# TensorE picks 23 more of 832 gathered columns: a graph network kernel on one core of Trainium2

## The reference, cut to what matters

```python
msg = H[src] * norm[:, None]
out = jax.ops.segment_sum(msg, dst, num_segments=n)          # GCN, three times
...
msg = diff @ tw.T + tb + phi[dst]                            # diff = x[src] - x[dst]
agg = jax.ops.segment_max(msg, dst, num_segments=x.shape[0]) # edge convolution, four times
```

## Time and profile before

| | us |
|---|---|
| median of 3 runs | 9450.62 (9448.05 to 9455.34) |
| the profiled execution | 9444.14 |
| its span, first to last instruction | 9442.3 |

### The profile page before, as it was taken

The page is one execution under the profiler, slowest core; times in us unless marked ns, Lnnn a source line. Parts: engine busy times, 40 slices in busy tenths (PEclk is TensorE's granted clock), DMA queues, the critical chain, the costliest instruction groups (busy, mean ns, idle before and its releaser), DMA issues. The chain is left out here.

```text
span 9442.3 us, 137452 instructions
## 1 busy us (share of the span) xinstructions
PE 1819.4 (19%) x9607; PEld 1531.1 (16%) x9607; DVE 3654.1 (39%) x20408; ACT 3485.0 (37%) x23810; POOL 6987.7 (74%) x6815
## 2 busy tenths in 40 slices
PE   2000057788884000020002000020002000020000
PEld 1000046777774000010001000010001000010000
DVE  4333344444443333333333333333334333333333
ACT  4444221111114444334442444334442444324441
POOL 5777668888883777777777777777776777777777
PEclk6555567777777555565556555565555555555555
DMA  6444535555553333333333333333334333333333
GB/s 214 161 159 158 190 79 77 77 77 77 75 72 111 108 108 112 110 108 108 113 111 111 111 109 108 113 105 112 108 110 138 103 117 111 109 108 110 108 112 128
DMA packets 483882, 1071.04 MB, mean 113 GB/s; under 512 B 162484, under 2 KB 293278, under 8 KB 428104
## 3 DMA queue, kind: packets, MB, share of 16 engines
q0 software_dynamic: 310432, 442.95, 21.5%
q1 hardware_dynamic: 169557, 619.06, 17.8%
q10 hardware_dynamic: 2940, 1.00, 0.1%
HBM read 511.83 MB, written 559.14 MB: 113 GB/s over the span
## 5 line engine op out<-in xcount | busy, mean ns | idle before, releaser
L1035 POOL DMA_INDIRECT WORK<-table,S x5502 | 5194.3, 944 | 1923.2 <-issue 1689.0
L1071 DVE COPY FE<-XF 128x4 uint8 x9856 | 1311.1, 190 | 3271.9 <-issue 1824.8
L1114 ACT COPY FE<-XF 128x4 uint8 x20608 | 2101.3, 191 | 1104.6 <-issue 1092.0
L1134 ACT COPY WORK<-psum 128x512 f32<-128x512 f32 (+1 forms) x1456 | 846.3, 581 | 2874.1 <-DVE psum L1089 2864.6
L1304 POOL DMA_INDIRECT acc<-TOT,stage x832 | 1301.3, 1564 | 274.6 <-issue 209.7
L1089 DVE SCALAR_TENSOR_TENSOR psum<-psum,RESET,WORK 128x128 f32<-128x128 f32 x3320 | 1189.1, 358 | 493.3 <-DMA WORK<-table,S 426.8
L1154 PE MATMUL psum<-ident,FE 128*128 128x128 f32 x238 | 106.5, 447 | 6110.0 <-ACT FE L1114 4714.0
L1089 DVE SCALAR_TENSOR_TENSOR psum<-psum,KEEP,WORK 128x128 f32<-128x128 f32 x2490 | 896.9, 360 | 639.9 <-DMA WORK<-table,S 278.8
L1154 PEld LDWEIGHTS psum<-ident,FE 128*128 128x128 f32 x238 | 43.3, 182 | 6172.5 <-issue 5903.0
L1438 ACT COPY TOT<-psum 128x512 f32<-128x512 f32 x208 | 121.9, 586 | 1250.2 <-DMA acc<-TOT,stage 1245.0
L1509 DVE SCALAR_TENSOR_TENSOR BASE<-psum,WEIGHT,BASE 128x128 f32<-128x128 f32 x832 | 234.1, 344 | 761.9 <-PE psum L1379 761.8
(11 more groups left out here) (255 smaller groups left out, 2540.4 us busy)
## 6 DMA issues: line engine op xcount, KB each, us to landing
run_rows<-WORK SPq DMA_DIRECT2D x357, 1024.0 KB, 4.2
WORK<-table SPq DMA_DIRECT2D x10752, 0.5 KB
WORK<-table,S POOLq DMA_INDIRECT x5502, 2.6
fill_rows<-BASE SPq DMA_DIRECT2D x52, 1024.0 KB, 6.8
WORK<-fill_rows SPq DMA_DIRECT2D x104, 512.0 KB, 3.7
table<-TF SPq DMA_DIRECT2D x56, 384.0 KB
WORK<-carry_rows SPq DMA_DIRECT2D x49, 384.0 KB, 6.6
acc<-TOT,stage POOLq DMA_INDIRECT x832, 3.3
```

The lines of the kernel that those rows point to most:

```text
L1035: pool.indirect_dma_start(RING_T[:, b * WIDE + k, :], None, table, table_row(table, INDEX[:, t:t + 1]))\
L1071: i = dve.tensor_copy(PICKED[:, s, e:e + 1].bitcast(u8), TT[:, ds(held_rows["dve"][e % 32], 4)])
L1114: i = act.copy(PICKED[:, j % 2, e:e + 1].bitcast(u8), TT[:, ds(held_rows["act"][e % 32], 4)])
L1134: act.copy(RING_T[:, t % SPAN:t % SPAN + n, :], CHAINED[:, t % PSUM_COLS:t % PSUM_COLS + n, :])\
```

## The change

23 more columns (BY_PE: 63, 95, ... 767) leave GpSimd's list. TensorE makes them: for each edge a product of the identity with the column of `XF` at a register's address, whose 128 x 1 result goes into one column of bank 6 or 7. It does 16 edges per quad, 32 registers loaded at a time. When 128 are there (`built_p`), ScalarE copies the bank into `PICKED` (`drawn`), and from there the column goes the way of the other picked ones: a transpose, and ScalarE's copy into the ring. The transposes now use bank 5 alone, so that each waits for the copy of the one before it, and the chain's ring in PSUM shrinks from 24 to 20 columns. TensorE's loop now runs over the quads, with the picks of a quad ahead of the transposes that are due there. The edges' addresses of BY_PE are in units of float32 columns, not bytes.

```diff
-PSUM_COLS = 24
+PSUM_COLS = 20
...
-FROM_TT = sorted(BY_ACT + BY_DVE)
-AWAY = BY_ACT + BY_DVE + BY_SP
+BY_PE = [t for t in range(63, 772, 32)]
+FROM_TT = sorted(BY_ACT + BY_DVE + BY_PE)
+AWAY = BY_ACT + BY_DVE + BY_PE + BY_SP
...
-                for k, (t, size) in enumerate([(t, 4) for t in BY_ACT + BY_DVE] + [(t, 4 * F) for t in BY_SP]):
+                for k, (t, size) in enumerate([(t, 4) for t in BY_ACT + BY_DVE] + [(t, 1) for t in BY_PE] + [(t, 4 * F) for t in BY_SP]):
...
                 for q in range(quads):
                     pick_edges(q)
+                    for j, col in enumerate(BY_PE):
+                        if q == col // QUAD - 3:
+                            act.wait_ge(built_p, j + 1)
+                            wait(act, off_turned, FROM_TT.index(BY_PE[j - 2]) + 1 if j > 1 else 0)
+                            act.copy(PICKED[:, 4 + j % 2, :], bank(6 + j % 2)[:, 0:P]).then_inc(drawn, 1)
                     for j, col in enumerate(FROM_TT):
                         if q == col // QUAD - 2:
                             c = col // WIDE
                             act.wait_ge(off_turned, j + 1)
                             wait(act, stored[c % RING], c // RING * 16)
-                            act.copy(RING_T[:, col % SPAN, :], bank(6 + j % 2)[:, 0:P]).then_inc(homed, 1)
+                            act.copy(RING_T[:, col % SPAN, :], bank(5)[:, 0:P]).then_inc(homed, 1)
...
-                for j, col in enumerate(FROM_TT):
-                    wait(pe, homed, j - 1)
+
+                def pick_edges(q):
+                    for j, col in enumerate(BY_PE):
+                        first = (q - (col // QUAD - P // EDGES - 3)) * EDGES
+                        if not 0 <= first < P:
+                            continue
+                        if first == 0:
+                            wait(pe, drawn, j - 1)
+                        if first % 32 == 0:
+                            held_rows["pe"] = row_offsets(mybir.EngineType.PE, len(BY_ACT) + len(BY_DVE) + j,
+                                                          first, 32, 1)
+                        for e in range(first, first + EDGES):
+                            m = nc.tensor.matmul(bank(6 + j % 2)[:, e:e + 1], ident[:],
+                                                 XF[:, ds(held_rows["pe"][e % 32], 1)], start=True, stop=True)
+                        if first + EDGES == P:
+                            m.then_inc(built_p, 1)
+
+                def turn(j, col):
+
+                    wait(pe, homed, j)
                     if col in BY_ACT:
                         k = BY_ACT.index(col)
                         s = k % 2
                         pe.wait_ge(built_a, k + 1)
-                    else:
+                    elif col in BY_DVE:
                         k = BY_DVE.index(col)
                         s = 2 + k % 2
                         pe.wait_ge(built_v, k + 1)
-                    nc.tensor.transpose(bank(6 + j % 2)[:, 0:P], PICKED[:, s, :], ident[:]).then_inc(off_turned, 1)
+                    else:
+                        k = BY_PE.index(col)
+                        s = 4 + k % 2
+                        pe.wait_ge(drawn, k + 1)
+                    nc.tensor.transpose(bank(5)[:, 0:P], PICKED[:, s, :], ident[:]).then_inc(off_turned, 1)
+
+                for q in range(quads):
+                    pick_edges(q)
+                    for j, col in enumerate(FROM_TT):
+                        if q == col // QUAD - 3:
+                            turn(j, col)
```

More of the change, by code:

```diff
@@ L273, in gnn_kernel @@
         tt_turned, tt_copied = sem("tt_turned"), sem("tt_copied")
-        built_a, built_v = sem("built_a"), sem("built_v")
+        built_a, built_v, built_p = sem("built_a"), sem("built_v"), sem("built_p")
+        drawn = sem("drawn")
         off_turned, homed = sem("off_turned"), sem("homed")
@@ L1181, in fetch @@
                         for a in range(first, first + n, 32):
-                            rows = row_offsets(mybir.EngineType.SP, len(BY_ACT) + len(BY_DVE) + j, a, 32, 4 * F)
+                            rows = row_offsets(mybir.EngineType.SP, len(AWAY) - len(BY_SP) + j, a, 32, 4 * F)
                             for e in range(32):
```

## The result

The changed kernel takes 11,912.72 us (median of 4 runs, 11,911.87 to 11,916.88) against 9449.33 us before in the same runs: a ratio of 1.2607, 95% interval 1.2585 to 1.2629. The forecast was 11,820. The profiled execution took 11,916.88 us, its span 11,915.1.

The account below looks back on a forecast made before the run. GpSimd's gathers, 1.25 us apart, were taken to bound the kernel. With TensorE at 55.8 us a column, six passes grow 343 us, the first 310: 9444 + 2370 + 2 = 11,816, said as 11,820; range 9,900 to 13,100.

Parts of the forecast that it names:

- The bound before: GpSimd's gathers bound all seven passes, 1.25 us each; 23 fewer save 28.7 us a pass, 201 us in all.
- the first rival: TensorE keeps up at the upper clock level and gathers stay the bound: 9243 us; chance 0.16.
- Two loads an edge set the pace, 0.427 us: TensorE's new products: two weight loads each pace an edge even with one column moving; 54.6 us a column.
- The level stays low: TensorE's clock stays at its lower level, near 0.50, through a pass, as one column moves per product.
- The column's 55.8 us: TensorE's time per new column: 54.6 us of loads plus 1.2 of transposes and round trip, against 36.25 of gathers.
- the round trip: TensorE's wait at single bank 5 for ScalarE's copy between two transposes: some 0.45 + 0.26 us a column.
- the register loads: TensorE's four loads of 32 registers a column, 1.98 us each: hidden behind queued products, 7.9 us if open.
- The sum: One pass: column 767 comes at 1298 us, the pass ends at 1328, against 984.6.
- the end of a pass: Behind column 767: a 4.2 us store, 16 gathers (20 us), 4.2 to L1157, some 2 of copy, step and lift.
- The second: Rival: upper level, but TensorE's sequencer lags or the level is up part-time; about 11,000, or from 9,500 on; chance 0.11.
- The third: Rival: TensorE keeps the stationary operand, no load between products; the first rival's time, within its 0.16.

Follow-up runs that it names:

- e3: Changed kernel with each product moving 128 copies of its column (broadcast) in place of one: 9279.10 us, ratio 0.982.
- e4: Changed kernel with TensorE making the products of every second edge only, the other 64 of a column left out: 9276.97 us, ratio 0.9818.
- e6: e3 without SP's 12 row-by-row fetched columns, which go back to GpSimd in every pass: 9305.00 us, ratio 0.986.
- e10: e3 with SP's 12 fetched columns given back to GpSimd in the first pass alone: 9216.47 us, ratio 0.9769.
- e2: Changed kernel with TensorE taking one column in 64, 12 columns in place of 23: 9362.53 us, ratio 0.991.
- e5: Changed kernel with only the identity's first 64 columns as stationary operand, upper 64 features left out: 9267.09 us in one execution.
- e8: Changed kernel with two turning banks in place of one and a ring of 16 columns: 11,831.35 us, ratio 1.2521.

## Why the prediction was right, point by point

**The bound before.** Right for six passes: with 23 gathers fewer and TensorE fast enough (e3, e4) they fall from 984.6 to 957.7 us on average, 27 of the 28.7 forecast. Wrong for the first, which I counted among the seven: it was 1017.9 us before and 1021 in e3 and is bound by SP's fetches (e6, e10). The 1017.9 of the earlier trace rows stood there, 33 us above the other six and 37 above the gathers' 981, and I passed it over. That is why the first rival's 9243 would have been some 9282 (six passes at 27 are 162 us off 9444; e3 took 9279), and most of what e2 missed (12 gathers are 15 us, and its first pass, at 1018.9 us, did not give them).

**Two loads an edge set the pace, 0.427 us.** Right: 0.212 us a load in the timeline, no idle time ahead, and e5 shows that it is the load's columns. The step that carried the forecast was that the two loads set the pace of a product whether 49 columns move or one; it came from one row, L746.

**The level stays low.** Right, 0.50 in every pass, and e3 bears out the reason given: with 128 columns moved per product the mean is 0.87 to 0.88. The rule of the Trainium skill that I set against the rows ("TensorE: Matmul & The Clock Gate", "LDWEIGHTS (loading the stationary operand)": a load as its columns over 1.2 GHz, 107 ns) doesn't hold for float32 here: at 0.50 a load took 212 ns for 128 columns and 108 ns for 64 (e5), so a float32 column is loaded at half of that rate. Only with the clock at 1.00 did 128 columns come near the figure, at 113 ns (e3). TensorE was loading weights for 1271 of the 1341 us of a pass, and the level stayed where it was; the first rival needed the upper one.

**The column's 55.8 us.** Right: 256 loads are 54.4 us, and in pass three the products of one column start 55.6 to 56.3 us behind those of the one before from the third column on; the last transpose, column 767's, is loaded 1299.6 us after the first gather (1298 forecast). Of the parts, the round trip is 0.5 in place of 0.7 us (e8), and the register loads are hidden, as taken. The trace shows with what: TensorE's sequencer makes an edge's address (FUSED_REGOPS on L1163, one an edge) up to 3.75 us ahead of the edge's first load, nearly nine edges of 0.427 us, and a register load of 2.2 us fits into that lead. The passage that the prediction cites for it ("Architectural detail" in the Trainium skill) says of weight loads, not of register loads, that they are pulled ahead; by an estimate from these times the lead is some 35 loads and matmuls, and a depth of 64 was not seen.

**The sum.** 1328 us a pass were forecast, 1341 came, and 1354 in the first. The term that was sized too small is the end of a pass. The timeline of the changed kernel there:

```profile
6071.02 18.29 SPq L1219 DMA_DIRECT2D WORK<-table  x49
...
6077.18 0.59 ACT L1141 COPY WORK<-psum 128x512 f32<-128x512 f32 x1 [0.53 <-DVE psum L1091]
...
6084.72 0.95 POOL L1037 DMA_INDIRECT WORK<-table,S  x1 [0.31 <-issue]
6089.37 27.85 SPq L1201 DMA_DIRECT2D run_rows<-WORK  x7
6090.46 13.26 DVE L1091 SCALAR_TENSOR_TENSOR psum<-psum,RESET,WORK 128x128 f32<-128x128 f32 x32 [5.43 <-DMA WORK<-table]
...
6093.53 0.94 POOL L1037 DMA_INDIRECT WORK<-table,S  x1 [7.86 <-DMA run_rows<-WORK]
...
6116.51 0.18 PEld L1192 LDWEIGHTS psum<-ident,WORK 128*128 128x128 f32 x1 [41.42 <-DVE WORK L1091]
```

Column 767's quad is lifted by 6077.8, but SP's queue issues the store only at 6089.37, behind 64 row-by-row fetches of column 788 (L1219; the view begins within them, in all they take 23 us), on which VectorE waits too. GpSimd, done with the quarter before at 6085.7, begins its last 16 gathers at 6093.53, 7.9 us later. The store of the quarter before had met the other 64 fetches of that column: it went out at 6061.8, 2.5 us after its last quad was lifted. I had written that SP's fetches and stores are moved past nothing. Once TensorE sets the time, the store stands on the path with whatever is ahead of it in SP's queue: from the forecast's 1298 on a pass takes 43 us in place of 30. By an estimate from these rows some 10 of the 13 us are the two waits, and 1.6 are TensorE's later end. Six times 13 and 25 in the first pass are 103 us, which is all of the 101 by which the profiled execution lies above the 11,816. This is read from the timeline; no run leaves the fetches out of the changed kernel, and the 25 of the first pass are not taken apart (there 8.9 us lie between the last gather and L1192, in place of 4.2).

**The rivals.** The first (TensorE keeps up, and the gathers bind) is what e3 and e4 show in six of their seven passes; the change as it was made does not. The second (a sequencer that can't follow) is excluded at the lower level by e5 and at the upper one by e3, whose edges come every 0.23 us. The third (the operand is kept) is excluded by the count of loads, 41,216.

## What to carry to other kernels

Cost a TensorE product by its weight load when few columns move: in these runs a float32 product with a stationary operand of 128 columns took two loads of 0.21 us at the clock's lower level, with one column moving as with 49. An idle engine's share says nothing of what a new kind of work will cost it: multiply the count by the nearest row and hold it against the period of what binds now. And if the clock's level is what decides, columns that cost nothing (a broadcast operand beside a load as long) can be a cheap way to it, as in e3.

## What the runs showed of the hardware that I had not expected

That one edit turns a loss of 26% into a gain of 1.8%: moving 128 copies of a column in place of one, for products whose loads are as long anyway, brings the mean clock of a pass from 0.50 to 0.88 (e3). After a wait of 10 us the next 32 loads took 5.06 us in place of 3.65: the level was 1.00 ahead of the wait, 0.50 at the start of these loads and 1.00 behind them. And register loads of 2.2 us, hidden entirely behind products of 0.212 us a load, come into the open by some 0.3 to 0.5 us at 0.113 (the waits marked "issue" between e3's loads). In the trace the sequencer's lead over loads at that pace is at most 1.9 us, again some eight and a half edges, and a register load takes longer than that (2.1 us).
